# Looking up and signalling the first expert's token numbers chunk by chunk

## The reference, cut to what matters

```python
n_tok = b * s                         # 4096
k = n_tok // E                        # 512 tokens for each of 8 experts
logits = xf @ Wr + br
Sm = softmax(logits)
G_t, idx_t = top_k(Sm.T, k)           # every expert picks its 512 tokens
tokens = xf[idx]                      # rows gathered by token number
mid = silu(einsum('keh,ehf->kef', tokens, Wu) + bu)     # 256 -> 682
out = einsum('kef,efh->keh', mid, W_down) + b_down      # 682 -> 256
y = zeros_like(xf).at[idx].add(G[..., None] * out)      # rows added back
```

## Time and profile before

| | us |
|---|---|
| median of 3 runs | 711.85 (709.07 to 712.37) |
| the profiled execution's own time | 706.99 |
| its span in the trace | 705.3 |
| PE busy | 641.8 (91%) |
| DVE busy | 423.1 (60%) |
| ACT busy | 302.5 (43%) |
| POOL busy | 267.1 (38%) |
| mean granted clock of PE, share of full | 0.974 |

### The profile page before, as it was taken

The page is one execution under the profiler, slowest core; times in us unless marked ns, Lnnn a source line. Parts: engine busy times, 40 slices in busy tenths (PEclk is TensorE's granted clock), DMA queues, the critical chain, the costliest instruction groups (busy, mean ns, idle before and its releaser), DMA issues.

```text
span 705.3 us, 14454 instructions
## 1 busy us (share of the span) xinstructions
PE 641.8 (91%) x5191; PEld 465.9 (66%) x5191; DVE 423.1 (60%) x1287; ACT 302.5 (43%) x632; POOL 267.1 (38%) x390
## 2 busy tenths in 40 slices
PE   7899999899999988879999999998899999992991
PEld 5465565677777755567656665657888888882881
DVE  6654766798999658872112222112668988883672
ACT  2323324777888824543221222220555555510660
POOL 4201102454455512043465445233211334355475
PEclk9999999999999999999999999999999999996896
DMA  8649862777884318941563884323713494123562
GB/s 265 215 133 221 201 137 76 119 127 125 136 134 80 107 48 211 362 133 47 100 146 40 254 267 109 70 30 40 230 60 121 151 317 156 61 91 107 176 188 79
DMA packets 92878, 99.95 MB, mean 142 GB/s; under 512 B 13782, under 2 KB 82905, under 8 KB 92804
## 3 DMA queue, kind: packets, MB, share of 16 engines
q1 hardware_dynamic: 83592, 82.57, 43.8%
q0 software_dynamic: 9216, 16.46, 10.4%
HBM read 61.20 MB, written 38.05 MB: 141 GB/s over the span
## 4 chain that ended last, share of the span: by engine, by line
PE 49%; DVE 5%; DMA 3%; issue 2%; POOL 1%; ACT 1%; POOLq 0%; SPq 0%; DVEq 0%; ACTq 0%
PE pc L1707 10%; PE pc L1684 9%; PE pc L2543 4%; PE pc L2276 4%; PE pc L2271 3%; PE pc L2312 2%; PE pc L1061 2%; PE pc L2269 2%; PE pc L1660 2%; PE pc L2253 2%; PE pc L1703 2%; DMA y<-in_ctxT 1%; PE pc L61 1%; PE pc L2334 1%; PE pc L1672 1%
## 5 line engine op out<-in xcount | busy, mean ns | idle before, releaser
L1524 POOL DMA_INDIRECT scratch_resid<-y,k_idx x32 | 54.9, 1716 | 81.8 <-DVE y L1592 81.5
L502 DVE TENSOR_REDUCE neg_max<-pb_two 128x8 f32<-128x1024 f32 x64 | 78.0, 1219 | 11.9 <-PE pb_two L832 8.8
L667 ACT ACTIVATE probs<-pb_two,b_key_cols 128x1024 f32<-128x1024 f32 x64 | 76.9, 1201 | 17.4 <-PE pb_two L856 17.4
L1707 PE MATMUL pc<-w_dn,mid 128*128 128x256 f32 x320 | 73.3, 384 | 0.0
L1635 ACT ACTIVATE mid<-pc,b_up 128x512 f32<-128x512 f32 x35 | 24.0, 687 | 109.7 <-PE pc L1684 109.7
L1707 PEld LDWEIGHTS pc<-w_dn,mid 128*128 128x128 f32 x320 | 59.5, 190 | 12.7 <-issue 5.3
L1684 PE MATMUL pc<-gT,w_up 128*128 128x512 f32 x140 | 61.2, 592 | 0.0
L1592 DVE TENSOR_SCALAR y<-pc,gate 128x256 f32<-128x256 f32 x32 | 15.5, 483 | 66.7 <-PE pc L1707 50.0
L1515 POOL DMA_INDIRECT rows<-scratch_rows,k_idx x32 | 32.0, 1001 | 51.7 <-DVE k_idx L1374 39.0
L1684 PEld LDWEIGHTS pc<-gT,w_up 128*128 128x128 f32 x140 | 26.6, 190 | 30.5 <-issue 30.1
L1574 DVE COPY gT<-pc 128x512 f32<-128x512 f32 x7 | 4.8, 691 | 61.1 <-PE pc L1672 61.1
(11 more groups left out here) (382 smaller groups left out, 1410.5 us busy)
## 6 DMA issues: line engine op xcount, KB each, us to landing
qs<-scratch_qparts SPq DMA_DIRECT2D x48, 128.0 KB, 4.1
ks<-scratch_kparts SPq DMA_DIRECT2D x48, 128.0 KB
w_dn<-in_W_down SPq DMA_DIRECT2D x8, 640.0 KB
scratch_slots<-s_zero SPq DMA_DIRECT2D x1, 4160.0 KB, 23.2
cT<-in_ctxT SPq DMA_DIRECT2D x8, 512.0 KB, 6.0
s_x<-in_x SPq DMA_DIRECT2D x8, 512.0 KB, 6.9
scratch_rows<-s_x SPq DMA_DIRECT2D x16, 256.0 KB, 4.4
scratch_resid<-s_x SPq DMA_DIRECT2D x8, 512.0 KB, 5.8
```

Source lines behind the costliest of these rows:

```text
L502: V.tensor_reduce(neg_max[:].rearrange("p (b u j) -> p u b j", b=2, u=2)[:, u], ps_both[0][:].rearrange("p (b j k) -> p b j k", b=2, j=4), ...
L667: A.activation(probs[t % 2 * 2 + u][:], ps_both[1][:].rearrange("p (h q) -> p h q", h=HEADS // 2), ACT.Exp, bias=key_cols[:, 1, t:t + 1], ...
L1524: pool.indirect_dma_start(out=T["resid"], out_offset=bass.IndirectOffsetOnAxis(ap=S["idx"][:, e, c:c + 1], axis=0), in_=y[e % 2][:, c, :], ...
L1707: ins = nc.tensor.matmul(here(c), mid[e % 2][m][:, c * P:(c + 1) * P], w_dn[e % 2][:, m, :], start=False, stop=(m == MT - 2))
```

## The change

- On DVE, the steps of experts 0 to 3 are followed at once by expert 0's tiles (128 columns instead of the 256 of experts 0 and 1). Expert 0's four look-ups follow, and behind each of them one instruction makes that chunk's column of token numbers and raises `idx_s`. The steps of experts 4 to 7 are moved behind expert 0's second chunk, expert 1's tiles behind its last.
- On PE, expert 0's four products come first and raise `look_ps` by 1; those of experts 1 to 3 follow.
- On POOL, each gather of expert 0 waits for its own chunk. Expert 1's wait for `idx_s` 5, the others' for 7.

```diff
-        for g in range(2):
+        def steps_of(g):
             V.tensor_scalar(reach[:, g, :], ramp[:], start_col[:, g:g + 1], None, ALU.is_ge).then_inc(step_s, 1)
-        first_two, others = slice(0, 2), slice(2, E)
-        tiles_behind(first_two)
-        dve.wait_ge(tiles_s, 1)
-        V.tensor_reduce(tiles[:, first_two, :], behind[:, first_two], AX.X, ALU.add).then_inc(tiles_s, 1)
-        dve.wait_ge(tiles_s, 2)
-        V.tensor_scalar(tiles[:, 1:2, :], tiles[:, 1:2, :], float(P), P / 2.0, ALU.mult, ALU.add).then_inc(tiles_s, 1)
+        def tiles_of(e):
+            tiles_behind(slice(e, e + 1))
+            dve.wait_ge(tiles_s, 2 * e + 1)
+            V.tensor_reduce(tiles[:, e:e + 1, :], behind[:, e:e + 1], AX.X, ALU.add).then_inc(tiles_s, 1)
...
-        look(0)
-        dve.wait_ge(found_d, 4)
-        V.scalar_tensor_tensor(S["idx"][:, 0, :], tiles[:, 0, :], float(P), inside[:, 0, :], ALU.mult, ALU.add).then_inc(idx_s, 1)
-        dve.wait_ge(tiles_s, 3)
+        steps_of(0)
+        tiles_of(0)
+        dve.wait_ge(look_ps, 1)
+        for c in range(CAP // P):
+            look_chunk(0, c)
+            dve.wait_ge(tiles_s, 2)
+            dve.wait_ge(found_d, c + 1)
+            V.scalar_tensor_tensor(S["idx"][:, 0, c:c + 1], tiles[:, 0, c:c + 1], float(P), inside[:, 0, c:c + 1],
+                                   ALU.mult, ALU.add).then_inc(idx_s, 1)
+            if c == 1:
+                steps_of(1)
+        tiles_of(1)
+        dve.wait_ge(tiles_s, 4)
+        V.tensor_scalar(tiles[:, 1:2, :], tiles[:, 1:2, :], float(P), P / 2.0, ALU.mult, ALU.add).then_inc(tiles_s, 1)
+        dve.wait_ge(tiles_s, 5)
         dve.wait_ge(found_a, 4)
         V.scalar_tensor_tensor(S["idx"][:, 1, :], inside[:, 1, :], 0.5, tiles[:, 1, :], ALU.mult, ALU.add).then_inc(idx_s, 1)
...
-            for c in range(CAP // P):
-                for e in range(4 * g, 4 * g + 4):
-                    rows = slice(e % 4 * TT, (e % 4 + 1) * TT)
-                    ins = nc.tensor.matmul(ps[e][:, c * P:(c + 1) * P], reach[rows, g, c * P:(c + 1) * P], riseT[rows, g, :],
-                                           start=True, stop=True)
-            ins.then_inc(look_ps, 4)
+            for experts, done in (((0,), 1), ((1, 2, 3), 3)) if g == 0 else (((4, 5, 6, 7), 4),):
+                for c in range(CAP // P):
+                    for e in experts:
+                        rows = slice(e % 4 * TT, (e % 4 + 1) * TT)
+                        ins = nc.tensor.matmul(ps[e][:, c * P:(c + 1) * P], reach[rows, g, c * P:(c + 1) * P], riseT[rows, g, :],
+                                               start=True, stop=True)
+                ins.then_inc(look_ps, done)
...
-            pool.wait_ge(route.idx_s, e + 1 if e < 2 else 4)
+            if e:
+                pool.wait_ge(route.idx_s, ST + 1 if e == 1 else ST + 3)
             for c in range(ST):
+                if e == 0:
+                    pool.wait_ge(route.idx_s, c + 1)
```

More of the change, by code:

```diff
@@ L1351, in on_vector, with look_chunk @@
         dve.wait_ge(startT_s, 1)
-        for g in range(2):
+        def steps_of(g):
             V.tensor_scalar(reach[:, g, :], ramp[:], start_col[:, g:g + 1], None, ALU.is_ge).then_inc(step_s, 1)
-        first_two, others = slice(0, 2), slice(2, E)
-        tiles_behind(first_two)
-        dve.wait_ge(tiles_s, 1)
-        V.tensor_reduce(tiles[:, first_two, :], behind[:, first_two], AX.X, ALU.add).then_inc(tiles_s, 1)
-        dve.wait_ge(tiles_s, 2)
-        V.tensor_scalar(tiles[:, 1:2, :], tiles[:, 1:2, :], float(P), P / 2.0, ALU.mult, ALU.add).then_inc(tiles_s, 1)
+        def tiles_of(e):
+            tiles_behind(slice(e, e + 1))
+            dve.wait_ge(tiles_s, 2 * e + 1)
+            V.tensor_reduce(tiles[:, e:e + 1, :], behind[:, e:e + 1], AX.X, ALU.add).then_inc(tiles_s, 1)
+        def look_chunk(e, c):
+            V.tensor_scalar(junk_d[:, e // 2 % 2, c, :], ps[e][:, c * P:(c + 1) * P], place[:, c:c + 1], None, ALU.is_le, ALU.add,
+                            accum_out=inside[:, e, c:c + 1]).then_inc(found_d, 1)
         def look(e):
@@ L1365, in look @@
             for c in range(CAP // P):
-                V.tensor_scalar(junk_d[:, e // 2 % 2, c, :], ps[e][:, c * P:(c + 1) * P], place[:, c:c + 1], None, ALU.is_le, ALU.add,
-                                accum_out=inside[:, e, c:c + 1]).then_inc(found_d, 1)
-        look(0)
-        dve.wait_ge(found_d, 4)
-        V.scalar_tensor_tensor(S["idx"][:, 0, :], tiles[:, 0, :], float(P), inside[:, 0, :], ALU.mult, ALU.add).then_inc(idx_s, 1)
-        dve.wait_ge(tiles_s, 3)
+                look_chunk(e, c)
+        steps_of(0)
[13 more added lines that the diff above has]
+        dve.wait_ge(tiles_s, 5)
         dve.wait_ge(found_a, 4)
@@ L1376, in on_vector @@
             look(e)
-        tiles_behind(others)
+        tiles_behind(slice(2, E))
     def tiles_behind(experts):
@@ L1384, in last_tiles @@
     def last_tiles(dve):
-        dve.wait_ge(tiles_s, 4)
+        dve.wait_ge(tiles_s, 6)
         nc.vector.tensor_reduce(tiles[:, 2:, :], behind[:, 2:], AX.X, ALU.add).then_inc(tiles_s, 1)
-        dve.wait_ge(tiles_s, 5)
+        dve.wait_ge(tiles_s, 7)
         nc.vector.tensor_scalar(tiles[:, 3::2, :], tiles[:, 3::2, :], float(P), P / 2.0, ALU.mult, ALU.add).then_inc(tiles_s, 1)
     def last_places(dve):
-        dve.wait_ge(tiles_s, 6)
+        dve.wait_ge(tiles_s, 8)
         dve.wait_ge(found_d, 16)
```

## The result

The changed kernel takes 716.49 us in the median of 9 runs (711.96 to 718.93), the kernel before 711.36 (708.22 to 712.4, 9 runs). The ratio is 1.0076, interval 1.0051 to 1.0101: 5.4 us slower, where I had forecast 0.8 and given "slower by over 0.5%" 7 in 100. The profiled execution of after took 716.49 us, its span 714.3, mean granted clock 0.969 (before: 706.99, 705.3, 0.974).

What follows compares the result with a forecast made beforehand. DVE's own queue ahead of `xg` was taken as the bound, with gathers hidden. An earlier first look-up (-0.58) and a longer list (+3.14 against 1.74) gave +0.82, so 711.85 + 0.8 = 712.65 us; range 708.6 to 715.3.

Steps and rivals of the forecast that it cites:

- What bounds the kernel: Ahead of `xg`, DVE's own queue was the bound; gathered rows lay ready 0.56 and 0.39 us earlier, or more.
- rival A: Gathers bind `xg`, landing about 0.6 us later than recorded; earlier gathers give at most -1.4 us, 710.4; chance 0.06.
- DVE's list: DVE's instructions from the first `reach` to `xg` get longer, passed on in full: +0.82 us; chance 0.62.
- The gain of 0.58: Expert 0's first look-up on DVE starts at 304.63 instead of 305.21, waiting for four products only.
- my own 0.17 and 0.03: Delays in us: 0.17 until PE's product result is there, 0.03 until the dependent DVE step starts.
- forecast 3.14: DVE's time from first look-up to expert 2's: 1.84 look-ups, 0.40 `reach`, 0.90 expert 1's tiles and numbers; 1.74 before.
- my upper end of +1.46: Upper bound on DVE's delay: 0.82 plus 0.64, for dearer half-size instructions and columns holding up look-ups.
- what lies beside it: Work off DVE's chain: ACT's look-ups, PE's later products and turns, POOL's earlier gathers; all hidden, adding nothing.
- The first of my tests for being wrong: The forecast is wrong if DVE stands idle before `xg` and a DMA releases it.
- B: PE's clock fall before the first expert's products is missed, saving 1.65 us: -0.8 in all, 711.0; chance 0.12.
- C: PE's low clock lasts twice as long, over the first expert's products: +2.5 us, 714.3; chance 0.12.
- the sum's bounds: Ends for the delay of DVE's list from uncertain instruction costs and PE's pace: +0.4 to +1.46 us.

Runs made afterwards that it cites:

- e1_before: The kernel before, unchanged, run and profiled a second time: mean 710.3 us, ratio 0.9984.
- e8: The kernel before with extra identity turns, results unread, in every pause of PE in this stage: mean 709.7 us, ratio 0.9985.
- e17: The kernel before with expert 0's columns one by one, expert 1's tiles behind the last, each expert 0 gather waiting for its own column: 713.2 us, ratio 1.0021.
- e14: The changed kernel, but expert 0's gathers wait for all four columns, as before the change: mean 715.4 us, ratio 1.0076.
- e3: The changed kernel with PE's products in the old order, DVE's first look-up waiting for all sixteen: mean 714.3 us, ratio 1.0045.
- e5: The kernel before with only the second `reach` moved, behind expert 0's second look-up: mean 715.7 us, ratio 1.0072.
- e4: The changed kernel with the second `reach` back in its old place, right behind the first: mean 715.3 us, ratio 1.0053.
- e15: The kernel before with expert 0's token numbers made column by column and each of its gathers waiting for its own column: mean 716.3 us, ratio 1.0072.
- e1_after: The changed kernel, unchanged, run and profiled a second time: mean 714.5 us, ratio 1.0044.
- e9: The changed kernel with extra identity turns in PE's pauses, 5 of them between the two halves of the products: mean 715.9 us, ratio 1.0085.
- e11: The kernel before with each column of expert 0's token numbers behind its own look-up, gathers still waiting for all four: 709.5 us, ratio 0.9999.
- e2: The kernel before with only PE's order changed, expert 0's four products first; DVE waits for all sixteen: mean 712.4 us, ratio 1.0019.

## Why the prediction was wrong

**What bounds the kernel: right for the trace shown, not for every execution.** There DVE's own list, not the gathers, holds `xg`. But in e1_before, the same kernel, DVE waited 0.34 us for the rows and `xg` chunk 1 came at 9.97, not 9.37 (in e8 the wait is 0.43). The rows' lead of 0.39 to 0.56 us was thinner than a gather's scatter from one execution to the next, and rival A had some ground. An earlier gather alone gains little even so. In e17 POOL starts its first gather 3.69 us behind `reach` instead of 4.43, and nothing comes of it.

**DVE's list: the right sign, too small.** e14 has the changed DVE list, its first products at full clock, and no wait of DVE from the first look-up to `xg`:

```profile
303.91 0.49 DVE L1353 TENSOR_SCALAR reach<-ramp,start_col 128x512 f32<-128x512 f32 x1
...
305.97 0.35 DVE L1361 TENSOR_SCALAR_CACHE_REDUCE junk_d<-pc,place 128x128 bf16<-128x128 f32 x1 [1.06 <-PE pc L1458]
...
306.51 0.34 DVE L1361 TENSOR_SCALAR_CACHE_REDUCE junk_d<-pc,place 128x128 bf16<-128x128 f32 x1
...
309.64 0.35 DVE L1361 TENSOR_SCALAR_CACHE_REDUCE junk_d<-pc,place 128x128 bf16<-128x128 f32 x1
...
315.16 0.40 DVE L1570 TENSOR_SCALAR xg<-rows 128x256 f32<-128x256 f32 x1
```

- From `reach` to the first look-up 2.06 (forecast 304.63 - 303.09 = 1.54). The gain of 0.58 is 0.06. Expert 0's four products alone are ready 1.19 us behind the first of them (304.78 to 305.97); all sixteen in the old order took 1.24 in e1_before. The first 32 records took 1.72 us on PE, 1.17 in e3 with the old order. The Trainium skill, TensorE: Matmul & The Clock Gate, Part 3, The mechanism, says that a weight load overlaps products in flight only where its row group differs; these two rows agree. With my own 0.17 and 0.03 taken off, four in a row on the same partitions come to 0.25 each, an estimate, against the 0.116 that I took from the turns.
- From the first look-up to expert 2's 3.67 (forecast 3.14). One look-up with its column is 0.54 (305.97 to 306.51), not 0.46: the column starts 0.11 behind the end of the accumulator's read (306.25 + 0.08 = 306.33, 306.44), not 0.03 as I read from the one behind a row of four look-ups. That is 0.32 of the 0.53; the other 0.2 is that expert 2's look-up starts 0.29 behind expert 1's numbers (309.35 to 309.64), where I took 0.08. The half-size instructions (0.28, 0.29) and the moved `reach` were right.
- So `xg` chunk 1 comes at 11.25 instead of 9.37: +1.88, not +0.82, and over my upper end of +1.46. e17, with nearly this list (10.98) and little of the late completions, is 1.5 us slower on the mean. That is what this term passed on would give, though e17's interval holds 1.

**The step that failed: what lies beside it.** In the prediction's words: "PE's products of experts 4 to 7 now wait for the moved `reach` ... so it is hidden." I asked only whether they would be done in time by their records. e5 moves this `reach` alone and loses 4.8 us on the mean: PE's signals come 2.3 us behind the records in the profile of after and 4.2 us in that of e5. In the first pair of traces the 5.1 us of the stage divide so: 0.79 up to the first look-up (forecast -0.58; the products ran at the low clock), 1.93 up to expert 2's (forecast 1.40), 1.27 up to `xg` chunk 1 (forecast 0), where DVE stood still for the late second half, and 1.14 up to `gT` (forecast 0). The sentence quoted is where the assumption broke first, and not the cause: e4 and e15 lose as much with `reach` in its old place. Of the 5.4 us (3.1 by e1_after's ratio) the 1.9 of DVE's list leave 3.5 (1.2) for this. I had no rival for it: none of them lets PE's work be recorded in time and reported late. The first of my tests for being wrong was also the wrong one: DVE does stand idle in this stretch, but released by PE, not by a DMA.

**POOL.** The first gather of after started 4.48 us behind `reach` (forecast 3.0), 0.95 us behind the end of the first column as forecast; it is late since the first look-up is, at 2.91. In e9, where that comes at 2.06, it is 3.63.

**B and C, the clock.** C named the right sign and a piece of it: in after the low clock goes on for 6.8 us over the first products (x16: 5.08 us, 3.87). But e1_before has as long a low clock (309.64 to 316.46) without the loss, and in e15, as slow as after, the clock is up until 318.07, when the late completion is over; in e9 it fell behind the start of the crawl. So no run shows a part of the change's loss that is the clock's.

**The numbers.** The scatter was taken from four executions 5.4 us apart; later ones of the unchanged kernel lie up to 11 us apart, and 716.49 us is outside the range, which had no room for a case of +5 us. 0.88 for "the same" rested on the sum's bounds, that is, on the assumption that nothing outside the sum moves.

## What to carry to other kernels

On a chain that jumps from engine to engine, shortening one hop is worth what the *next* engine's list allows: here 0.06 us were gained in front and 1.9 paid behind (e14). Work that "is hidden" by its records may not be so by its signals: look for consumers that start long behind the records of what they wait for, and leave chance for it where a change shifts PE's small pieces. Where two edits tested alone cost nothing, test them together, and the other way round (e11, e15, e17).

## What the runs showed of the hardware

- PE's completions can be signalled 2 to 5 us behind the records, and turns that wait for nothing can start 0.7 to 1.4 us apart (e9), at full clock. Which kernels show it depends on placing: e11 and e15 differ in their code by what POOL's gathers wait for and by nothing else. In eight of the ten traces with the loss it ends within 0.3 us of the landing of the last of eight gathers.
- A comparison with an accumulator costs 0.27 in a row of its kind, and 0.54 with a one-column instruction that reads its result behind it (e14, e15).
- Sixteen 32-row products take 0.5 us longer with four in a row on the same partitions and then twelve over three groups than with all four groups in turn (look-up at 2.65 in e2, 2.11 in e1_before). The four in a row alone are ready no sooner (1.19 us, e14) than all sixteen in turn (1.24, e1_before).
- The same kernel's gathers can land 1 us later in one execution than in another: the first gather's last landing record is 3.0 us behind its start in the first trace of before, 4.0 in e1_before.
